# A small write and a wait on GpSimd in front of every indirect DMA of a graph network kernel

## The chip, the cores and the metric

The kernel runs on one core of a Trainium2 chip. The metric is the device time of one execution in microseconds (us). Before the change it is 4527.97 us, the median of three runs (4527.56 to 4528.97).

## What is computed

Four graph layers run one after the other on 6,250 nodes with 64 features and 200,000 edges; the edges come sorted by their target node. Each layer normalises its input and adds its result to `x`. Cut to what matters here:

```python
h = relu(layernorm(x)); Z = h @ W_shared.T; ze = he @ W_shared.T
a = Z[src] @ Wa_s.T + ze @ Wa_e.T + Z[dst] @ Wa_d.T       # one number per edge
H_all = einsum('ni,rio->nro', h, W_rel)                    # 16 relations
x = x + relu(segment_sum(H_all[src, rel] * a, dst))
h = relu(layernorm(x))
x = x + A @ relu(A @ h)            # A: sum over edges, two aggregations
h = relu(layernorm(x))
x = x + four_gcn_layers(h)         # four more aggregations, two dense pairs
h = relu(layernorm(x))
v_e = segment_sum(edge_attr, src) / max(count, 1)          # by SOURCE node
x = x + mlp(concat([h, v_e, u]))
```

## The kernel before

The work runs in five stages, and GpSimd's own work is almost only indirect DMAs.

1. **Setup.** TensorE computes the table `rel_table` (100,352 rows of 65 numbers: one row per node and relation) and SyncE stores it to device memory. GpSimd prepares two blocks of edge rows (`early_rows`).
2. **The edge loop.** The target nodes are cut in 391 groups of 16. TensorE sums group after group (`sum_group`, lines 1820 to 1832), from one-hot matrices that VectorE writes (lines 1350 and 1371); the same loop counts, for each pair of nodes, how many edges join them, and ScalarE stores these counts as the table `adjacency`. The rows of `rel_table` that the edges need are fetched by GpSimd: a round `r` is four gathers (`indirect_dma_start`, line 704), each of 128 rows, into a ring of 64 slots (`ring`, a part of the tile `ld_all`). There are 391 rounds, 1,564 gathers. Before round `r` GpSimd waits until group `r - 14` is summed (semaphore `summed`), so that its ring slots are free, and until the gathers of round `r - 2` have landed. VectorE needs round `g + 3` for group `g`. The ring therefore holds some nine rounds of lead. After the loop GpSimd writes the early rows to their places in `l3_sorted` (line 712, 64 indirect writes of 128 rows).
3. **Six aggregations.** `adjacency` is read back, in 13 pairs of halves for each aggregation, and multiplied with the node rows (line 1911); between them lie layer norms and two dense stages.
4. **Placing edge rows**, beside the aggregations and a part of stage 5. The fourth layer wants the edge rows by source node. The 200,000 rows come in blocks of 4,096: ScalarE and VectorE split a block in three bf16 parts (`split_high`, `split_middle`, `split_low`, lines 849 to 873), and GpSimd writes it with 32 indirect DMAs to computed places (line 730, 47 blocks, 1,499 writes; the last block has 27). GpSimd waits for `l3_split` before a block. Three buffers (`rows16`) take turns: ScalarE's `split_high` of block `m` waits until the writes of block `m - 3` have landed (`l3_moved`). ScalarE does these steps in fixed slots of its own program, between the copies of an aggregation's results, so a late write holds up the copies behind it.
5. **Node sums and the network.** The rows of `l3_sorted` are read back in two generations and summed by node (line 2029). The reading of the second generation waits for every placing write.

GpSimd's program is written out (no loop in it on this path), one instruction after the other. `Chain.link` adds one to a semaphore when its instruction is done and has the engine wait for that count before it goes on; the setup's instructions all use it. The tile `w_rel` holds the relation weights; its last reader is the computation of `rel_table`, and GpSimd waits for the storing of that table before its first gather.

Of the kernel before, what the change touches and what calls it, by code (L numbers as in the profile page):

```python
# [107 lines left out]
def build(nc, A, out):  # L108
# [3 lines left out]
    with ctx:  # L112
        def sb(name, shape, dt=f32):
            return ctx.enter_context(nc.sbuf_tensor(name, shape, dt))
# [30 lines left out]
        w_rel = sb("w_rel", [P, R, D])  # L145
# [183 lines left out]
        def s(name):  # L329
            if name not in S:  # L330
                S[name] = sem(name)
            return S[name]
# [290 lines left out]
        def _(pool):  # L623
            ch = Chain(pool, s("pool_chain"))
# [26 lines left out]
            def edge_pass(j):  # L651
# [5 lines left out]
                with pool.Fori(0, COUNT[j] // n) as i:  # L657
# [9 lines left out]
                    for k in range(n):  # L667
                        if name == "l3" and k % K == 0:
# [4 lines left out]
                                                (comb3[k] if name == "l3" else comb[k])[:, 0:width], None, compute_op=ALU.add,  # L673
                                                bounds_check=NROW - 1).then_inc(s(f"{fam}_scattered{k}"), 16)

            for n, (block, k0, cols, rows) in enumerate(early_rows):
                values = early_in[:, 0:cols * D48].rearrange("p (k d) -> p k d", d=D48)
                top = early_in[:, 0:cols * D48].bitcast(bf16).rearrange("p (k d two) -> p k d two", two=2, d=D48)[:, :, :, 1]
                pool.wait_ge(s("x_loaded"), 32 + 16 * (n + 1))
                pool.memset(rows[:, :, ONE:KEY], 1.0)  # L680
                for part in range(2):
                    ch.link(pool.tensor_copy(rows[:, :, part * D48:(part + 1) * D48], top))
                    ch.link(pool.tensor_tensor(values, values, rows[:, :, part * D48:(part + 1) * D48], ALU.subtract))
                pool.tensor_copy(rows[:, :, 2 * D48:3 * D48], top).then_inc(s("const_ready"), 1)
# [8 lines left out]
            with pool.If(flag1):  # L693
                pool.wait_ge(s("ring_ready"), 1)
                for r in range(ROUNDS):
                    if r * K == RING // 2:
                        pool.wait_ge(s("ring_ready"), 2)
                    if r >= AHEAD:
                        pool.wait_ge(s("summed"), r + TG - AHEAD)
                    if r >= 2:  # L700
                        pool.wait_ge(s(f"ring_in{r % 2}"), r // 2 * (16 * K))
                    pool.sem_inc(s("turn"), 1)
                    for c in range(r * K, r * K + K):
                        pool.indirect_dma_start(ring[:, c % RING, 0:TW], None, rel_table,  # L704
                                                bass.IndirectOffsetOnAxis(ap=rel_i[:, c:c + 1], axis=0)).then_inc(s(f"ring_in{r % 2}"), 16)
                pool.wait_ge(s("sorted_zeroed"), 16 * ZERO_DMAS)
                for block, k0, cols, rows in early_rows:
                    pool.wait_ge(s("l3_pos_ready"), block + 1)
                    pool.sem_inc(s("turn"), 1)
                    for k in range(cols):  # L710
                        at = block * SB_K + k0 + k
                        pool.indirect_dma_start(l3_sorted, bass.IndirectOffsetOnAxis(ap=l3_pos[:, at:at + 1], axis=0),
                                                rows[:, k, :], None).then_inc(s(f"l3_moved{block}"), 16)
            with pool.Else():
# [4 lines left out]
            with pool.If(flag2):  # L719
                pool.wait_ge(s("l3_pos_ready"), NSB + 1)  # L720
                for m in range(NSB + 1 - EARLY):
                    n = m + EARLY
                    q = m % 3
                    pool.wait_ge(s("l3_split"), m + 1)
                    if m < EARLY:
                        pool.wait_ge(s(f"l3_moved{m}"), 16 * SB_K)
                    pool.sem_inc(s("turn"), 1)
                    for k in range(SB_K if n < NSB else REST_DMAS):
                        parts = REST_TAIL if n == NSB and k == REST_K else P
                        pool.indirect_dma_start(l3_sorted, bass.IndirectOffsetOnAxis(ap=l3_pos[0:parts, n * SB_K + k:n * SB_K + k + 1], axis=0),  # L730
                                                rows16[q][0:parts, k, :], None).then_inc(s(f"l3_moved{q}"), 16)
            with pool.Else():
# [1343 lines left out]
```

## Time and profile before

| what | us |
|---|---|
| median of three runs | 4527.97 |
| span of the profiled execution | 6109.1 |
| its GpSimd busy time | 3104.2 |
| its TensorE busy time (matmul) | 3539.3 |
| its VectorE busy time | 2693.7 |

The profiled execution's span is the time from its first to its last instruction; no other time of that execution is recorded, and nothing is known of what lies around it. It is 1581.1 us (35%) longer than the median of the runs. Durations and orders are read from it, and the text says where that difference matters. "Issue" in a row is idle time for which the profile shows no releaser; a name behind an arrow is what ended the idle time.

### The profile page before, as it was taken

The numbers are of one execution on the slowest core, as the hardware profiler recorded it, in microseconds if no ns is written. First come the engines' busy times: TensorE is split into PE (matmuls) and PEld (weight loads), VectorE is DVE, ScalarE is ACT, GpSimd is POOL, SyncE is SP. The second block draws the span as 40 slices with busy tenths as digits, with TensorE's granted clock in tenths as the row PEclk, the third lists the DMA queues.
The fourth block names the chain that finished last, engine by engine and source line by source line (L and its number), as shares of the span: only waits on it lengthen the run. The fifth ranks groups of instructions, "written<-read, shape, count | busy, mean of one in ns | idle before, by whom it ended". The sixth has DMA issues, their size and how long they took to land.

```text
span 6109.1 us, 86298 instructions
## 1 busy us (share of the span) xinstructions
PE 3539.3 (58%) x18243; PEld 1786.5 (29%) x18244; DVE 2693.7 (44%) x9772; ACT 1506.8 (25%) x3741; POOL 3104.2 (51%) x3186
## 2 busy tenths in 40 slices
PE   5377777777776777776425455344654655451345
PEld 2133333333333333333202222122321223121333
DVE  6266666666666666666350110401202203015556
ACT  3132332323232323232111111111111111112552
POOL 2455555555555555555355656455255562555331
PEclk8588888888888888888656677676676775675668
DMA  5433333333333333333034444343143441342444
GB/s 181 105 77 79 77 77 77 79 77 78 77 79 77 82 73 79 77 77 76 25 114 148 149 140 168 127 137 125 58 167 129 155 154 61 128 157 93 158 153 111
DMA packets 599826, 650.58 MB, mean 106 GB/s; under 512 B 422854, under 2 KB 435892, under 8 KB 593429
## 3 DMA queue, kind: packets, MB, share of 16 engines
q1 hardware_dynamic: 382453, 463.07, 23.5%
q0 software_dynamic: 100064, 110.65, 8.6%
q10 hardware_dynamic: 117184, 75.50, 4.0%
q8 instruction: 42, 0.69, 0.0%
q14 instruction: 83, 0.68, 0.0%
HBM read 453.58 MB, written 192.06 MB: 106 GB/s over the span
## 4 chain that ended last, share of the span: by engine, by line
PE 38%; another core or an unknown queue 21%; issue 19%; DVE 11%; DMA 7%; ACT 2%; DVEq 1%; SPq 1%; POOL 0%; ACTq 0%; POOLq 0%
PE bank L1827 10%; PE bank L1828 7%; PE bank L1832 7%; PE bank L1911 7%; DMA ld_all<-adjacency 3%; DMA rel_table<-ld_all 2%; DVE hid_T L1652 2%; DMA rel_and_z<-adjacency 1%; DVE hid_T L1371 1%; PE bank L2029 1%; PE bank L1858 1%; DVE hid_T L1350 1%; PE bank L1961 1%; PE bank L1967 1%
## 5 line engine op out<-in xcount | busy, mean ns | idle before, releaser
L730 POOL DMA_INDIRECT l_sorted<-arena,l_pos x1499 | 1467.7, 979 | 1538.6 <-ACT arena L873 1057.8
L704 POOL DMA_INDIRECT ld_all<-rel_table,rel_and_z x1564 | 1537.4, 983 | 1158.3 <-remote 450.8
L1827 PE MATMUL bank<-hid_T 128*128 128x400 f16 x2346 | 974.6, 415 | 668.5 <-issue 549.4
L1828 PE MATMUL bank<-hid_T 128*128 128x384 f16 x2346 | 948.3, 404 | 28.7 <-issue 28.2
L1371 DVE TENSOR_SCALAR hid_T<-count_key,hid_T 128x400 f16<-128x400 int16 x2346 | 599.9, 326 | 744.9 <-remote 434.2
L1911 PE MATMUL bank<-rel_and_z,ld_all 128*128 128x512 fp8e4 (+1 forms) x1872 | 523.7, 419 | 524.7 <-issue 471.5
L1911 PE MATMUL bank<-ld_all 128*128 128x512 fp8e4 (+1 forms) x1950 | 504.6, 419 | 333.1 <-DMA ld_all<-adjacency 147.1
L1832 PE MATMUL bank<-ld_all,arena 128*32 x4692 | 519.6, 247 | 164.1 <-issue 163.3
L1827 PEld LDWEIGHTS bank<-hid_T 128*128 x2346 | 257.1, 110 | 1149.4 <-issue 1145.0
L793 ACT CAST ld_all<-bank 128x400 fp8e4<-128x400 f32 x391 | 191.1, 489 | 1595.4 <-remote 959.1
L1313 DVE COPY accT<-bank 128x512 f32<-128x512 f32 (+1 forms) x78 | 51.2, 657 | 1079.8 <-remote 593.1
L1832 PEld LDWEIGHTS bank<-ld_all,arena 128*32 128x32 f32 x4692 | 350.5, 122 | 413.2 <-issue 343.0
L1911 PEld LDWEIGHTS bank<-rel_and_z,ld_all 128*128 128x128 f16 x1872 | 186.8, 105 | 851.5 <-issue 704.0
L908 ACT COPY G<-bank 128x256 f32<-128x256 f32 (+1 forms) x78 | 28.1, 360 | 1508.2 <-remote 694.2
L1911 PEld LDWEIGHTS bank<-ld_all 128*128 128x128 f16 x1950 | 201.7, 109 | 610.3 <-issue 463.6
L1350 DVE TENSOR_SCALAR hid_T<-io,arena 128x256 f16<-128x256 f16 x1564 | 353.2, 292 | 0.1
L1828 PEld LDWEIGHTS bank<-hid_T 128*128 x2346 | 265.2, 113 | 203.6 <-issue 132.9
L2029 PE MATMUL bank<-ld_all,hid_T 128*128 128x145 bf16 x1188 | 130.4, 277 | 251.5 <-issue 105.5
L796 ACT ACTIVATE ld_all<-bank,minus_max 128x400 f16<-128x400 f32 x391 | 236.0, 603 | 0.0
L797 ACT ACTIVATE ld_all<-bank,minus_max 128x384 f16<-128x384 f32 x391 | 228.1, 583 | 0.0
L2029 PEld LDWEIGHTS bank<-ld_all,hid_T 128*128 128x128 bf16 x1188 | 110.5, 122 | 276.5 <-issue 276.4
L1264 DVE TENSOR_TENSOR dst_f<-dst_f,bank 128x512 f32<-128x512 f32 x96 | 60.3, 683 | 290.6 <-ACT arena L850 227.6
(302 smaller groups left out, 4366.0 us busy)
## 6 DMA issues: line engine op xcount, KB each, us to landing
ld_all<-adjacency SPq DMA_DIRECT2D x72, 1600.0 KB
rel_and_z<-adjacency SPq DMA_DIRECT2D x72, 1600.0 KB
l_sorted<-zeros SPq DMA_DIRECT2D x151, 424.0 KB
arena<-in_edge_attr SPq DMA_DIRECT2D x195, 256.0 KB
adjacency<-ld_all ACTq DMA_DIRECT2D x391, 100.0 KB
ld_all<-l_sorted SPq DMA_DIRECT2D x33, 1095.0 KB
rel_table<-ld_all SPq DMA_DIRECT2D x49, 520.0 KB, 3.6
ld_all<-rel_table,rel_and_z POOLq DMA_INDIRECT x1564
```

Source lines behind the costliest of these rows:

```text
L704: pool.indirect_dma_start(ring[:, c % RING, 0:TW], None, rel_table, bass.IndirectOffsetOnAxis(ap=rel_i[:, c:c + 1], axis=0)).then_inc(s(f" ...
L730: pool.indirect_dma_start(l3_sorted, bass.IndirectOffsetOnAxis(ap=l3_pos[0:parts, n * SB_K + k:n * SB_K + k + 1], axis=0), rows16[q][0:par ...
L793: act.copy(count_stage[:, 0:w0], b0[:, 0:w0], saturate=False)
L796: act.activation(over_junk[:, 0:w0], b0[:, 0:w0], ACT.Relu, bias=minus_max[:], accum_out=over[:, bass.ds(g * 2, 1)])
L797: act.activation(over_junk[:, w0:GW], b1[:, 0:GW - w0], ACT.Relu, bias=minus_max[:], accum_out=over[:, bass.ds(g * 2 + 1, 1)]).then_inc(s( ...
L1350: v.tensor_scalar(lo_ring[:, q * K + k, :], io256[:], lo_in[:, k0 + k:k0 + k + 1], None, ALU.is_equal)
L1371: v.tensor_scalar(pair_hot[q % 2][:, k, :], count_key[:], pair_in[q % 2][:, k:k + 1], None, ALU.is_equal)
L1827: pe.matmul(b0[:, 0:w0], low[:, 0:P], pair_hot[q % 2][:, k, 0:w0], start=k == 0, stop=k == CG - 1)
L1828: pe.matmul(b1[:, 0:GW - w0], low[:, P:2 * P], pair_hot[q % 2][:, k, 0:GW - w0], start=k == 0, stop=k == CG - 1)
L1832: ins = pe.matmul(half_sums[q // 4][:, q % 4 * TW:(q % 4 + 1) * TW], weights[q % 2][:, k, :], ring[:, bass.ds((first + k) & (RING - 1), 1) ...
L1911: ins = pe.matmul(bank[slot][:, 0:n * GN].rearrange("p (g d) -> p g d", d=GN), x16[:, t, :], a_half[side][:, 0:n, t // 2 * GN:(t // 2 + 1) ...
L2029: ins = pe.matmul(bank[n % 3][:, 0:KEY], node_hot[n % 2][:, k, :], sorted_in[n % 3][:, k, 0:KEY], start=k == 0, stop=k == CAPC[gen] - 1)
```

## The change

A function `pause` is added. It writes 16 zeros per partition into the first relation of `w_rel`, through `Chain.link`, so that GpSimd waits for its own write. It is called in front of each gather of the edge loop, each early placing write, and each placing write of the 47 blocks: 1,564 + 64 + 1,499 = 3,127 calls. The code of the other branches is untouched, and so are all other engines.

```diff
+            def pause():
+                ch.link(pool.memset(w_rel[:, 0:1, 0:16], 0))
+
...
                     for c in range(r * K, r * K + K):
+                        pause()
                         pool.indirect_dma_start(ring[:, c % RING, 0:TW], None, rel_table,
...
                     for k in range(cols):
                         at = block * SB_K + k0 + k
+                        pause()
                         pool.indirect_dma_start(l3_sorted, bass.IndirectOffsetOnAxis(ap=l3_pos[:, at:at + 1], axis=0),
...
                     for k in range(SB_K if n < NSB else REST_DMAS):
                         parts = REST_TAIL if n == NSB and k == REST_K else P
+                        pause()
                         pool.indirect_dma_start(l3_sorted, bass.IndirectOffsetOnAxis(ap=l3_pos[0:parts, n * SB_K + k:n * SB_K + k + 1], axis=0),
```

GpSimd's program in the edge loop, two rounds, before (`ld_all` is the ring; `rel_and_z` holds the row numbers; a wait in brackets stands in front of its instruction):

```order
89 L704 DMA ld_all<-rel_table,rel_and_z 128x65 [waits summed,ring_in1]
90 L704 DMA ld_all<-rel_table,rel_and_z 128x65 x3
91 L704 DMA ld_all<-rel_table,rel_and_z 128x65 [waits summed,ring_in0]
92 L704 DMA ld_all<-rel_table,rel_and_z 128x65 x3
```

and after, one round and the head of the next (`pool_chain` is the semaphore of `Chain.link`):

```order
169 L677 MEMSET w_rel 128x16 [waits summed,ring_in1]
170 L708 DMA ld_all<-rel_table,rel_and_z 128x65 [waits pool_chain]
171 L677 MEMSET w_rel 128x16
172 L708 DMA ld_all<-rel_table,rel_and_z 128x65 [waits pool_chain]
173 L677 MEMSET w_rel 128x16
174 L708 DMA ld_all<-rel_table,rel_and_z 128x65 [waits pool_chain]
175 L677 MEMSET w_rel 128x16
176 L708 DMA ld_all<-rel_table,rel_and_z 128x65 [waits pool_chain]
177 L677 MEMSET w_rel 128x16 [waits summed,ring_in0]
```

The round's own waits now stand in front of the first write of zeros, and every gather waits for the write before it.

GpSimd's program at a block of placing writes, before (`arena` holds the split rows, `l_pos` their places):

```order
880 L730 DMA l_sorted<-arena,l_pos 242176x146 [waits l3_split,l3_moved1]
881 L730 DMA l_sorted<-arena,l_pos 242176x146 x31
882 L730 DMA l_sorted<-arena,l_pos 242176x146 [waits l3_split]
```

and after:

```order
3405 L736 DMA l_sorted<-arena,l_pos 242176x146 [waits pool_chain]
3406 L677 MEMSET w_rel 128x16 [waits l3_split,l3_moved1]
3407 L736 DMA l_sorted<-arena,l_pos 242176x146 [waits pool_chain]
3408 L677 MEMSET w_rel 128x16
3409 L736 DMA l_sorted<-arena,l_pos 242176x146 [waits pool_chain]
```

What stood as 32 DMAs in a row is now 32 pairs of a write and a DMA.

## Rows read from the trace of the kernel before

**Rows 1.** The page: head, engine totals, 40 slices, shares of the chain.
```profile
span 6109.1 us, 86298 instructions
...
PE 3539.3 (58%) x18243; PEld 1786.5 (29%) x18244; DVE 2693.7 (44%) x9772; ACT 1506.8 (25%) x3741; POOL 3104.2 (51%) x3186
...
PE   5377777777776777776425455344654655451345
...
POOL 2455555555555555555355656455255562555331
PEclk8588888888888888888656677676676775675668
...
PE 38%; another core or an unknown queue 21%; issue 19%; DVE 11%; DMA 7%; ACT 2%; DVEq 1%; SPq 1%; POOL 0%; ACTq 0%; POOLq 0%
```

**Rows 2.** GpSimd's groups: busy us, mean ns, idle before, its releasers.
```profile
L704 POOL DMA_INDIRECT ld_all<-rel_table,rel_and_z x1564 | 1537.4, 983 | 1158.3 <-remote 450.8 <-issue 401.5 <-PE bank L1832 305.2
L730 POOL DMA_INDIRECT l_sorted<-arena,l_pos x1499 | 1467.7, 979 | 1538.6 <-ACT arena L873 1057.8 <-issue 480.7
L712 POOL DMA_INDIRECT l_sorted<-h,l_pos x32 | 31.3, 977 | 10.4 <-issue 10.4
```

**Rows 3.** Timeline of GpSimd: the first gather and the last placing write.
```profile
201.75 1.16 POOL L704 DMA_INDIRECT ld_all<-rel_table,rel_and_z  x1 [3.35 <-issue]
...
5982.03 0.90 POOL L730 DMA_INDIRECT l_sorted<-arena,l_pos  x1 [0.31 <-issue]
```

**Rows 4.** Engines' busy time in three stretches of one aggregation.
```profile
core 0: us, PE busy (x) PEld busy (x) DVE busy (x) ACT busy (x) POOL busy (x), PEclk, DMA share, GB/s
3950.00:3980.00 30.00, 25.77 (x123) 12.32 (x122) 5.06 (x8) 7.49 (x10) 13.91 (x15) 0.97 0.73 261
3990.00:4040.00 50.00, 11.88 (x23) 2.50 (x21) 4.37 (x7) 7.52 (x10) 38.10 (x40) 0.53 0.15 45
4060.00:4090.00 30.00, 28.21 (x135) 13.49 (x133) 5.06 (x8) 8.40 (x12) 4.85 (x5) 0.98 0.73 256
```

**Rows 5.** Timeline of TensorE, the same aggregation.
```profile
3961.66 5.56 PE L1911 MATMUL bank<-ld_all 128*128 128x512 fp8e4 x25
...
4016.91 0.58 PE L1911 MATMUL bank<-rel_and_z,ld_all 128*128 128x512 fp8e4 x1 [2.21 <-issue]
4019.71 0.58 PE L1911 MATMUL bank<-rel_and_z,ld_all 128*128 128x512 fp8e4 x1 [2.22 <-issue]
```

**Rows 6.** GpSimd's groups from 500 to 2500 us, in the edge loop.
```profile
L704 POOL DMA_INDIRECT ld_all<-rel_table,rel_and_z x1154 | 1135.5, 984 | 863.4 <-remote 333.2 <-issue 293.7 <-PE bank L1832 236.6
```

**Rows 7.** GpSimd's waits at the placing writes: us in total, times, longest.
```profile
POOL l_sorted L730 <- ACT arena L873: 1057.8, 42, 100.2
```

**Rows 8.** Timeline of the edge loop, 1508 to 1516 us.
```profile
1508.40 1.49 DVE L1371 TENSOR_SCALAR hid_T<-count_key,hid_T 128x400 f16<-128x400 int16 x6 [2.41 <-remote]
...
1509.18 1.06 POOL L704 DMA_INDIRECT ld_all<-rel_table,rel_and_z  x1 [2.21 <-remote]
...
1510.54 0.99 POOL L704 DMA_INDIRECT ld_all<-rel_table,rel_and_z  x1 [0.30 <-issue]
1510.63 0.95 DVE L1350 TENSOR_SCALAR hid_T<-io,arena 128x256 f16<-128x256 f16 x4
...
1511.84 0.94 POOL L704 DMA_INDIRECT ld_all<-rel_table,rel_and_z  x1 [0.30 <-issue]
...
1513.09 0.95 POOL L704 DMA_INDIRECT ld_all<-rel_table,rel_and_z  x1 [0.31 <-issue]
```

**Rows 9.** Timeline of GpSimd's setup, every instruction waited for.
```profile
2.44 0.20 POOL L633 MEMSET ones<- 128x128 f32 x1
2.71 0.10 POOL L634 MEMSET minus_max<- 128x1 f32 x1
2.87 0.47 POOL L635 IOTA count_key<- 128x400 int16 x1
```

## Prediction, made before the changed kernel was run

> **What bounds the kernel now.** I read the page first. No engine is full: TensorE 58%, GpSimd 51%, VectorE 44% of the span [rows 1]. But the span is 6109.1 us and the median of the runs 4527.97. That is the main difficulty here: GpSimd's busy 3104 us are half of the one and 69% of the other. So I ask next whether the profiled execution has delays that cannot all be in a timed run. It has: "another core or an unknown queue" holds 21% of the chain that ended last (1283 us), and "issue" 19% [rows 1].
>
> The engines' busy time by stretch shows where. Between 3990 and 4040 us GpSimd issues placing writes without a pause (40 in 50 us), and TensorE gets only 23 matmuls through, though in the 30 us before and in 30 us soon after it does 123 and 135 [rows 4]. Its timeline shows matmuls 2.8 us apart, each after 2.2 us of "issue", where it did 25 in 5.56 us before [rows 5]. The DMA engines are at 0.15 then and cannot be full. The reader is to see that GpSimd keeps its pace (40 in 50 us is one in 1.25) while TensorE loses it. Whether these delays belong to the recording or to the chip no row tells; the 1581 us by which the timed runs are shorter say that most of them are absent there. I go by that.
>
> Last I read GpSimd's groups. A gather takes 0.983 us, a placing write 0.979, an early one 0.977 [rows 2]. Behind one another they stand 0.30 us apart [rows 8], so GpSimd needs 1.28 us for each. This pace is the same inside and outside the delayed stretches. If it holds in a timed run, then:
>
> - before the first gather: 201.75 us [rows 3]
> - 1,564 + 64 + 1,499 = 3,127 DMAs x 1.28 = 4003 us
> - behind the last placing write, 6109.1 - 5982.9 = 126 us [rows 1, 3]
> - sum 4331 us.
>
> The timed runs take 4528. Only 197 us are left for all of GpSimd's waits. In the profiled execution they were far more: it waits in the edge loop, where a round of four gathers comes every 2000 / (1154 / 4) = 6.93 us [rows 6] against 4 x 1.28 = 5.12 of its own, and 42 times for 1057.8 us at ScalarE's split, 25 us each [rows 7]. Take TensorE's delays away, and just these two waits shrink. My reading is that the timed kernel is paced by GpSimd's row of DMAs, in the loop and in the placing, though the profile shows it half idle.
>
> **The change, part by part.** It adds 3,127 writes of zeros with a wait, and removes and moves nothing else. The trace before has no such write between two DMAs, so I bound it. A memset of one element per partition takes 0.10 us, of 128 elements 0.20 [rows 9]; by a line through both, 16 elements take 0.11. In the setup, where each instruction is waited for, the next begins 0.06 to 0.07 us after the end [rows 9]. The 0.30 us in front of a DMA exist already [rows 8].
>
> - Least: the write disappears in those 0.30 us, so 0.
> - Middle: 0.07 us behind the DMA, 0.11 for the write, then the same 0.30, so +0.18.
> - Most: 0.30 on both sides of the write, so +0.41. A still larger cost would need the lock of the third rival.
>
> I take +0.18, since rows show each piece of it. On GpSimd alone that is 3,127 x 0.18 = 563 us (0 to 1282). By part:
>
> - Edge loop: 1,564 x 0.18 = 282 us; a round goes from 5.12 to 5.84 us. Queued behind the pause stand the gathers, and behind these VectorE's adding of the source term, the weights and TensorE's group sum. The ring's lead of nine rounds covers a few late rounds, not 391 of them.
> - Early writes: 64 x 0.18 = 12 us, behind the last gather, while the loop's tail and the second flag are computed (GpSimd waits there anyway); free, or 12.
> - Placing: 1,499 x 0.18 = 270 us; a block goes from 41 to 46.7 us. Behind a late block stand ScalarE's `split_high` three blocks on, then the copies of aggregation results behind it in ScalarE's program, and with them TensorE.
>
> What hides a part of it are the 197 us of waits. Some cannot shrink: the wait for the second flag, and the last block's wait for its split. I take half, 100 us, as giving way. Sum: 4528 + 563 - 100 = 4991. With all 197 absorbed it is 4894, with none 5091. Against the profiled execution's own span the same sum comes out near nothing: 5.84 is under 6.93 and 46.7 is under 41 + 25, so there all pauses but those of the last block (27 x 0.18 = 5 us) lie in idle time. Its span should stay near 6109, or fall if TensorE's delays follow the density of GpSimd's DMAs.
>
> **A rule against the rows.** In the loop a gather that starts while VectorE writes its six count one-hots takes 1.06 us, one beside no such work 0.94 [rows 8]. The sum uses the means, which hold that 0.1 already. The Trainium skill, "SBUF — State Buffer", section "Who interferes with whom", says that a VectorE instruction in a 2-port mode and a GpSimd instruction shut each other out of the shared port for the whole instruction. [...] By that rule a gather beside these instructions would wait for them, and the row's 0.1 us does not bear that out for a gather; a write of zeros no row shows.
>
> **The rivals.**
>
> 1. *The pause lies under cover (chance 0.17).* If everything in a timed run is shorter than in the trace by the same factor, 4528 / 6109 = 0.74, then the relations of the profile hold: GpSimd waits a quarter of every round, and the pauses fill that. Price: the last block alone, 5 us by the trace's durations, so 4533, no change. For it speaks the idle time in rows 6 and 7; against it that nothing shows a DMA of GpSimd below 0.94 us.
> 2. *Fewer delays on the other side (0.13; the one that is faster).* Suppose that TensorE's slow stretches [rows 4, 5] are in part in the timed runs, and come from GpSimd's DMAs standing too close. The pause would thin them from one in 1.28 us to one in 1.46. This can only pay if GpSimd's own pace is shorter in a timed run, so that TensorE and not GpSimd sets the end. A tenth of the 1283 us of unknown waits, 128 us, would give 4400. It decides from the point where the delays that go exceed the 0.18 us per DMA that GpSimd adds. Against it: by the trace's durations only 197 us can be had at all.
> 3. *The write waits for VectorE (0.07).* In a round VectorE has two stretches of such work, 1.49 and 0.95 us [rows 8]. If two of four writes fall into them and wait half of each, a round costs 0.75 + 0.48 = 1.2 us more, 391 x 1.2 = 480 on top: 4991 + 480 = 5471. This is the case that the Trainium skill's rule of the section named above would give for a write. Against it: the gathers beside the same stretches lose 0.1 us.
>
> **How the numbers follow.** Forecast, GpSimd paces and the pause is paid for: 0.63. With rival 3 that makes slower by over 0.2%: 0.70. Same: 0.17. Faster: 0.13. (0.2% is about what a measurement of this kernel can tell from no change.) Predicted time 4990. The forecast's own range, from a pause of 0.05 to one of 0.3 us, is 4528 + 156 - 100 = 4584 to 4528 + 938 - 0 = 5466. The range should leave out the faster case and the far end of a 0.41 us pause, and take in rival 1: 4515 to 5450.
>
> **What the next profile would show.** Right, if: the writes of zeros stand at 0.1 to 0.15 us, 3,127 of them; two DMAs of GpSimd begin about 1.46 us apart; GpSimd's idle time at the gathers and placing writes shrinks by as much as the writes add, with the span of the profiled execution hardly longer; and the timed runs come nearer to the span. Wrong, if: DMAs still begin 1.28 us apart (no cost), the DMA itself grows or shrinks behind a pause (then the sum is off in its main term), writes beside lines 1350 and 1371 take a microsecond (rival 3), or TensorE's matmuls of line 1911 are no longer spread in the bursts and the timed runs are shorter (rival 2). The forecast falls as a whole if the time stays within 10 us of 4528 while the distance between DMAs has grown: then GpSimd did not pace the timed kernel.

## The result, and the profile after

The changed kernel takes 4781.11 us (median of four runs, 4779.42 to 4785.0) against 4528.47 before: 252.6 us more, a ratio of 1.0557 (95% interval 1.0542 to 1.0572). I had forecast 4990, slower.

First the page of the changed kernel: head, engine totals, GpSimd's slices, TensorE's clock, shares of the chain that ended last, by engine and by line. In the changed kernel a gather is line 708, a block write line 736, the write of zeros line 677.

```profile
span 4780.5 us, 89425 instructions
...
PE 3231.5 (68%) x18243; PEld 1682.0 (35%) x18244; DVE 2770.8 (58%) x9772; ACT 1514.4 (32%) x3741; POOL 3498.2 (73%) x6313
...
POOL 2377777877787778777877777777757777577760
PEclk8699999998999999999967978688588785795778
...
POOL 44%; PE 19%; issue 16%; DVE 10%; DMA 7%; ACT 2%; DVEq 2%; POOLq 0%; SPq 0%; ACTq 0%
POOL l_sorted L736 24%; POOL ld_all L708 13%; PE bank L1833 5%; POOL w_rel L677 5%; PE bank L1838 4%; PE bank L1834 3%; DMA ld_all<-rel_table,rel_and_z 3%; DMA rel_table<-ld_all 2%; DVE hid_T L1658 2%; POOL l_sorted L717 1%; DVE hid_T L1377 1%; PE bank L1967 1%; PE bank L2035 1%; PE bank L1973 1%; DMA ld_all<-l_sorted 1%
```

GpSimd is busy in 73% of the span and holds 44% of the chain; in [rows 1] it held 0%. The span, 4780.5 us, lies 1.7 us below that run's own time. So this profile shows the timed kernel, while the one I predicted from (span 6109.1) did not: its execution was disturbed. The kernel before was therefore profiled twice more. One of these pages, to be held against [rows 1]:

```profile
span 4528.7 us, 86298 instructions
...
POOL 2377777777777777777667777777657777577650
...
PE 29%; POOL 23%; issue 12%; DVE 10%; DMA 3%; ACT 2%; DVEq 1%; SPq 0%; POOLq 0%; ACTq 0%
POOL l_sorted L730 22%; PE bank L1827 9%; PE bank L1832 6%; PE bank L1828 5%; PE bank L1911 2%; DVE hid_T L1652 2%; PE bank L1961 1%; PE bank L2029 1%; PE bank L1967 1%; DMA ld_all<-l_sorted 1%; DMA ld_all<-adjacency 1%; PE bank L1858 1%; DVE hid_T L1371 1%; DVE G L1520 0%; DVE hid_T L1350 0%
```

The span is 4528.7 us (the third one's 4524.2). GpSimd holds 23% of the chain, "another core or an unknown queue" nothing. Of the 23%, 22 are block writes (line 730), and the gathers of line 704 are not listed; in the changed kernel the gathers hold 13%. All comparisons below use this second profile of before.

Waits for other work, in total us, times and longest, of the kernel before (answering to [rows 7]) and of the changed one. The first line of each is ScalarE's wait for the placing writes, in front of `split_high`:

```profile
ACT arena L862 <- DMA l_sorted<-arena,l_pos: 293.1, 17, 29.7
...
POOL l_sorted L730 <- ACT arena L873: 132.9, 9, 43.6
...
POOL ld_all L704 <- PE bank L1832: 38.7, 39, 2.2
POOL ld_all L704 <- DMA ld_all<-rel_table,rel_and_z: 36.6, 120, 0.3
```

```profile
ACT arena L868 <- DMA l_sorted<-arena,l_pos: 489.8, 22, 33.5
...
POOL w_rel L677 <- ACT arena L879: 86.6, 6, 32.2
...
POOL ld_all L708 <- PE bank L1838: 11.6, 43, 0.3
```

The placing is later for ScalarE: it waits 489.8 us for placing writes where it waited 293.1. These rows do not give GpSimd's slack. A gap of 0.30 us stands in front of every DMA; the 120 waits for earlier gathers, 36.6 us, are this gap and nothing more, and some long waits stand under "issue". The slack is what is left of the span when GpSimd's own work is taken off. Before, that is 200.2 us up to the first gather, 3037.0 of DMAs, 3,127 x 0.30 = 938.1 of gaps and 109.8 behind the last write, 4285.1 in all; 243.6 us are left. The prediction had 197.

After the change the same terms are 202.3, 3050.8, 3,127 x 0.28 = 875.6 and 107.9, and the writes of zeros add 409.1, 4645.7 in all; 134.8 are left. So GpSimd's own work grew by 361 us, and 109 us of slack gave way.

GpSimd's groups of the second profile (busy us, mean ns, idle before), against [rows 2], and those of the changed kernel:

```profile
L704 POOL DMA_INDIRECT ld_all<-rel_table,rel_and_z x1564 | 1500.7, 960 | 560.9 <-issue 485.6 <-PE bank L1832 38.7 <-DMA ld_all<-rel_table,rel_and_z 36.6
L730 POOL DMA_INDIRECT l_sorted<-arena,l_pos x1499 | 1472.8, 983 | 599.0 <-issue 466.0 <-ACT arena L873 132.9
```

```profile
L708 POOL DMA_INDIRECT ld_all<-rel_table,rel_and_z x1564 | 1516.8, 970 | 461.2 <-POOL w_rel L677 407.2 <-issue 40.6 <-PE bank L1838 11.6
L736 POOL DMA_INDIRECT l_sorted<-arena,l_pos x1499 | 1471.1, 981 | 441.3 <-POOL w_rel L677 411.9 <-issue 29.4
L677 POOL MEMSET w_rel<- 128x16 f32 x3127 | 409.1, 131 | 92.1 <-ACT arena L879 86.6 <-DMA rel_table<-ld_all 2.6
```

The timeline of GpSimd in a block of placing writes (start, length, work, idle before), before and after:

```profile
3000.05 0.97 POOL L730 DMA_INDIRECT l_sorted<-arena,l_pos  x1 [0.31 <-issue]
3001.32 0.97 POOL L730 DMA_INDIRECT l_sorted<-arena,l_pos  x1 [0.30 <-issue]
```

```profile
2999.72 0.97 POOL L736 DMA_INDIRECT l_sorted<-arena,l_pos  x1 [0.28 <-POOL w_rel L677]
3000.69 0.12 POOL L677 MEMSET w_rel<- 128x16 f32 x1
3001.09 0.97 POOL L736 DMA_INDIRECT l_sorted<-arena,l_pos  x1 [0.28 <-POOL w_rel L677]
```

From one DMA to the next are 1.37 us, where it was 1.27. The write begins when the DMA ends, takes 0.12, and the next DMA begins 0.28 after it. The prediction had 1.46.

When the gathers and the blocks' writes began (least, median and longest time in ns, then the starts of the first and the last), and how long VectorE waited for gathers (us, times), before and after:

```profile
L704 POOL DMA_INDIRECT ld_all<-rel_table,rel_and_z x1564: 942/947/1286, 200.2 to 2257.5; - x196
...
  DVE rel_and_z L1356: 14.7, 6
...
L730 POOL DMA_INDIRECT l_sorted<-arena,l_pos x1499: 903/972/2871, 2358.8 to 4418.0; - x188
```

```profile
L708 POOL DMA_INDIRECT ld_all<-rel_table,rel_and_z x1564: 949/952/1348, 202.3 to 2390.2; - x196
...
  DVE rel_and_z L1362: 173.4, 81
...
L736 POOL DMA_INDIRECT l_sorted<-arena,l_pos x1499: 905/974/3277, 2482.0 to 4671.7; - x188
```

| stretch, first start to last start | before | after | difference |
|---|---|---|---|
| up to the first gather | 200.2 | 202.3 | +2.1 |
| gathers | 2057.3 | 2187.9 | +130.6 |
| early writes, second flag | 101.3 | 91.8 | -9.5 |
| blocks' writes | 2059.2 | 2189.7 | +130.5 |
| behind the last write | 110.7 | 108.8 | -1.9 |

The sum is 251.8 us, the whole difference. Half lies in the edge loop, half in the placing. In the loop VectorE now waits 173.4 us for gathers, where it waited 14.7.

Two stretches of 50 us of the changed kernel in which GpSimd issues all the time, to be held against the middle one of [rows 4]:

```profile
core 0: us, PE busy (x) PEld busy (x) DVE busy (x) ACT busy (x) POOL busy (x), PEclk, DMA share, GB/s
2985.00:3035.00 50.00, 29.46 (x165) 16.90 (x163) 5.16 (x9) 9.87 (x14) 39.98 (x73) 0.81 0.50 155
3900.00:3950.00 50.00, 28.10 (x114) 13.22 (x114) 4.97 (x8) 9.47 (x15) 39.98 (x73) 0.74 0.41 123
```

TensorE gets 165 and 114 matmuls through where the disturbed execution had 23.

TensorE's granted clock also fell, from a mean of 0.867 (0.97 between 500 and 2200 us) to 0.839 (0.93). In the loop this cannot be the cause, since GpSimd's own work fills the longer round almost by itself (below). In the placing what the lower clock costs was not tried apart.

### The profile page after: what moved, and what is told of

It is laid out like the page before. It is cut to its first block, busy times and chain, and to the rows that moved or that the text cites. A ratio compares the mean times of both kernels' runs of the same rounds, so it can differ in the third digit from the quotient of the medians.

```text
span 4780.5 us, 89425 instructions
## 1 busy us (share of the span) xinstructions
PE 3231.5 (68%) x18243; PEld 1682.0 (35%) x18244; DVE 2770.8 (58%) x9772; ACT 1514.4 (32%) x3741; POOL 3498.2 (73%) x6313
## 4 chain that ended last, share of the span: by engine, by line
POOL 44%; PE 19%; issue 16%; DVE 10%; DMA 7%; ACT 2%; DVEq 2%; POOLq 0%; SPq 0%; ACTq 0%
POOL l_sorted L736 24%; POOL ld_all L708 13%; PE bank L1833 5%; POOL w_rel L677 5%; PE bank L1838 4%; PE bank L1834 3%; DMA ld_all<-rel_table,rel_and_z 3%; DMA rel_table<-ld_all 2%; DVE hid_T L1658 2%; POOL l_sorted L717 1%; DVE hid_T L1377 1%; PE bank L1967 1%; PE bank L2035 1%; PE bank L1973 1%; DMA ld_all<-l_sorted 1%
## 5 line engine op out<-in xcount | busy, mean ns | idle before, releaser
L708 POOL DMA_INDIRECT ld_all<-rel_table,rel_and_z x1564 | 1516.8, 970 | 461.2 <-POOL w_rel L677 407.2
L1833 PE MATMUL bank<-hid_T 128*128 128x400 f16 x2346 | 861.2, 367 | 386.7 <-DVE arena L1386 253.3
L1834 PE MATMUL bank<-hid_T 128*128 128x384 f16 x2346 | 830.3, 354 | 0.0
L1377 DVE TENSOR_SCALAR hid_T<-count_key,hid_T 128x400 f16<-128x400 int16 x2346 | 674.8, 355 | 25.8 <-PE bank L1838 15.2
L1917 PE MATMUL bank<-ld_all 128*128 128x512 fp8e4 (+1 forms) x1950 | 475.2, 408 | 188.5 <-DMA ld_all<-adjacency 114.3
L1833 PEld LDWEIGHTS bank<-hid_T 128*128 x2346 | 236.1, 101 | 879.4 <-issue 873.1
L677 POOL MEMSET w_rel<- 128x16 f32 x3127 | 409.1, 131 | 92.1 <-ACT arena L879 86.6
L1917 PE MATMUL bank<-rel_and_z,ld_all 128*128 128x512 fp8e4 (+1 forms) x1872 | 410.2, 378 | 78.8 <-DMA rel_and_z<-adjacency 78.8
L1834 PEld LDWEIGHTS bank<-hid_T 128*128 x2346 | 239.3, 102 | 112.8 <-issue 33.3
L1926 PE MATMUL bank<-work,accT 128*128 128x64 f32 x588 | 83.5, 288 | 240.5 <-DVE accT L1319 240.5
L1270 DVE TENSOR_TENSOR dst_first<-dst_first,bank 128x512 f32<-128x512 f32 x90 | 56.4, 682 | 274.5 <-ACT arena L856 274.3
```

Source lines behind the costliest of these rows:

```text
L677: ch.link(pool.memset(w_rel[:, 0:1, 0:16], 0))
L1377: v.tensor_scalar(pair_hot[q % 2][:, k, :], count_key[:], pair_in[q % 2][:, k:k + 1], None, ALU.is_equal)
L1833: pe.matmul(b0[:, 0:w0], low[:, 0:P], pair_hot[q % 2][:, k, 0:w0], start=k == 0, stop=k == CG - 1)
L1834: pe.matmul(b1[:, 0:GW - w0], low[:, P:2 * P], pair_hot[q % 2][:, k, 0:GW - w0], start=k == 0, stop=k == CG - 1)
L1917: ins = pe.matmul(bank[slot][:, 0:n * GN].rearrange("p (g d) -> p g d", d=GN), x16[:, t, :], a_half[side][:, 0:n, t // 2 * GN:(t // 2 + 1) ...
```

## The experiments

All times are medians; "before" is 4527.5 to 4528.5 in each set.

### The kernel before, once more

No edit.

> The kernel before, unchanged, once more with its profile. Theory (the long span of its first profile, 6109 us, comes with the recording, and GpSimd's dense DMAs bring it about): the time is 4528 us and the profile is again far longer, over 5500 us, with TensorE's matmuls of line 1911 some 2 to 3 us apart while GpSimd writes. Rival (that first profile was a chance event): the span is within 30 us of the time, and TensorE's matmuls stand close.

4529.5 us (ratio 1.0003, 0.9993 to 1.0013) and a span of 4528.7. The theory that the long span comes with every recording of this kernel fell; the rival held. A later look for the same question:

> The kernel before, unchanged, for a third profile. Theory (the first profile's 6109 us were an event of that one execution, the second had 4528.7): the span is within 20 us of 4528. Rival (it recurs in some of the profiled executions): over 5500.

One run of 4525.98 us, span 4524.2. Of three profiled executions of before one was long; what disturbed it stays open.

### Where the pause costs: gathers alone, writes alone

```diff
# gathers alone: pause() only here
                     for c in range(r * K, r * K + K):
+                        pause()
# writes alone: pause() only in the two loops of placing writes
```

> The pause in front of the 1,564 gathers alone. In the changed kernel a pause adds 0.10 us between two DMAs (1.28 to 1.38). Theory (GpSimd paces both the loop and the placing): 1,564 x 0.10 = 156 us less a little slack, 4528 + 140 = 4670 us. Rival (only the placing is paced by GpSimd, the loop by VectorE and TensorE): 4528 to 4540. Rival (only the loop is): 4528 + 253 = 4780.

4639.63 us, +111.5 (ratio 1.0241, 1.0224 to 1.0258).

> The pause in front of the 1,563 placing writes alone (early ones and blocks). Theory (GpSimd paces both): 1,563 x 0.10 = 156 us less the waits that give way, some 40: 4528 + 115 = 4643 us. Rival (only the loop is paced by GpSimd): 4528 to 4540. Rival (only the placing): 4780.

4663.75 us, +135.6 (ratio 1.0301, 1.0284 to 1.0319). Both stages pay, the gathers less than the 140 us expected, the writes more than the 115; the parts sum to 247 of the 253 us. Neither rival, that a single stage pays, holds. With the pause at the gathers alone the loop's stretch grows by 133.5 us (2190.8 against 2057.3), and some of that comes back before the end.

### Two pauses in a row

```diff
+                ch.link(pool.memset(w_rel[:, 0:1, 0:16], 0))
                 ch.link(pool.memset(w_rel[:, 0:1, 0:16], 0))
```

> Two pauses in a row in front of each of the 3,127 DMAs. The second costs its write, 0.12 us, and the gap of 0.07 us between two chained instructions, with nothing left to hide it: +0.19 us each. Theory (GpSimd paces throughout): 4781 + 3,127 x 0.19 = 5375 us. Rival (a pause only shifts DMAs, the number does not count): 4781 to 4850. Rival (the chained write is longer in a pair because of VectorE's lock): over 5500.

5320.42 us (ratio 1.1751, 1.1732 to 1.1771), 539 above the changed kernel: 0.172 us for each second pause, against 0.081 for each first. Timeline of GpSimd:

```profile
3000.63 0.98 POOL L737 DMA_INDIRECT l_sorted<-arena,l_pos  x1 [0.28 <-POOL w_rel L678]
3001.61 0.13 POOL L677 MEMSET w_rel<- 128x16 f32 x1
3001.79 0.11 POOL L678 MEMSET w_rel<- 128x16 f32 x1
3002.18 0.98 POOL L737 DMA_INDIRECT l_sorted<-arena,l_pos  x1 [0.28 <-POOL w_rel L678]
```

DMAs stand 1.55 us apart. The second write adds its 0.11 and the 0.05 between the two. The distance grows by 0.18 (1.55 less 1.37), near the expected 0.19. Part is still absorbed: GpSimd's wait for ScalarE's split falls from 86.6 to 37.9 us.

### Write without wait, wait without write

```diff
 # no wait: the write waits for the one before it, the DMA for nothing
-                ch.link(pool.memset(w_rel[:, 0:1, 0:16], 0))
+                pool.wait_ge(s("pool_chain"), ch.base + ch.k)
+                ch.also(pool.memset(w_rel[:, 0:1, 0:16], 0))
 # wait alone
-                ch.link(pool.memset(w_rel[:, 0:1, 0:16], 0))
+                pool.sem_inc(s("pool_chain"), 1)
+                ch.k += 1
+                pool.wait_ge(s("pool_chain"), ch.base + ch.k)
```

> The 3,127 writes stay, but the DMA behind one no longer waits for it; each write waits only for the write before it, which has long been done. Theory (what a pause costs is the write's own 0.125 us in GpSimd's row, and the 0.27 us in front of the DMA are there with or without a wait): 4781 us within 10. Rival (the wait costs its part): under 4740. Rival (the DMA overlaps the write): 4528 to 4600.

> No writes: GpSimd's queue adds one to the semaphore itself and waits for that count, in front of each of the 3,127 DMAs. Theory (the wait lies inside the 0.30 us that stand between two DMAs anyway): 4528 to 4545 us, DMAs still 1.26 to 1.28 us apart. Rival (a wait alone costs some 0.05 us each): 4528 + 150 = 4680 or more.

The write without its wait: 4541.38 us, +13.9 (ratio 1.0031, 1.002 to 1.0043). The wait without a write: 4530.88, +3.4 (ratio 1.0005, 0.9996 to 1.0014). For the first, the theory of 4781 fell and the rival of an overlap (4528 to 4600) held; for the second the theory held, and its 3.4 us are not clear of noise. Neither half costs much alone. The second is not the same wait: here GpSimd's queue raises the count itself, in the pause the finished write does. Timelines of GpSimd, without wait, then without write:

```profile
3001.58 0.97 POOL L737 DMA_INDIRECT l_sorted<-arena,l_pos  x1 [0.18 <-issue]
3002.55 0.12 POOL L678 MEMSET w_rel<- 128x16 f32 x1
3002.86 0.97 POOL L737 DMA_INDIRECT l_sorted<-arena,l_pos  x1 [0.18 <-issue]
```

```profile
3001.57 0.97 POOL L738 DMA_INDIRECT l_sorted<-arena,l_pos  x1 [0.31 <-POOLq L677]
3002.85 0.97 POOL L738 DMA_INDIRECT l_sorted<-arena,l_pos  x1 [0.30 <-POOLq L677]
```

Both keep 1.27 to 1.28 us from DMA to DMA. The DMA begins 0.30 us after a DMA, but 0.18 after a write that it does not wait for, so a write of 0.12 is free: 0.12 + 0.18 = 0.30. If it waits for the write, the gap is 0.28 again. The 0.10 us that a pause adds from DMA to DMA are what the wait takes away again (0.28 less 0.18).

### A wide write, with and without the wait

```diff
-                ch.link(pool.memset(w_rel[:, 0:1, 0:16], 0))
+                ch.link(pool.memset(w_rel[:, 0:4, :], 0))        # or the form without a wait
```

> The changed kernel with a wider write: 256 zeros per partition in place of 16, waited for as before. By the rows of the setup (0.10 us for 1 element, 0.20 for 128) the write takes about 0.31 us in place of 0.125. Theory (what is waited for stands in GpSimd's row in full): 4781 + 3,127 x 0.185 = 5360 us. Rival (the cost is that of the wait, whatever the write's length): 4781 to 4800.

> The same wide write, but the DMA behind it does not wait for it. With the small write and no wait, the write lay inside the 0.30 us between two DMAs and cost 14 us in all. Theory (these 0.30 us are the start of the next DMA, and run beside whatever GpSimd does meanwhile): 0.31 us of writing just fills them, DMAs 1.28 to 1.35 us apart, 4540 to 4700 us. Rival (the start of the DMA begins when the write is done): as with the wait, over 5200.

With the wait 5366.04 us (ratio 1.1848, 1.183 to 1.1866), 6 us from the theory; the rival fell. Without it 5048.58 (ratio 1.1153, 1.1136 to 1.117), between theory and rival: both missed. Timelines, with the wait, then without:

```profile
3000.66 0.98 POOL L736 DMA_INDIRECT l_sorted<-arena,l_pos  x1 [0.28 <-POOL w_rel L677]
3001.64 0.33 POOL L677 MEMSET w_rel<- 128x256 f32 x1
3002.24 0.98 POOL L736 DMA_INDIRECT l_sorted<-arena,l_pos  x1 [0.28 <-POOL w_rel L677]
```

```profile
3001.48 0.97 POOL L737 DMA_INDIRECT l_sorted<-arena,l_pos  x1 [0.17 <-issue]
3002.45 0.33 POOL L678 MEMSET w_rel<- 128x256 f32 x1
3002.94 0.97 POOL L737 DMA_INDIRECT l_sorted<-arena,l_pos  x1 [0.17 <-issue]
```

The write takes 0.33 us. Then come 0.27 to 0.28 us with the wait and 0.16 to 0.17 without, close to the 0.28 and 0.18 of the small write. So the write stands in GpSimd's row in full, and what is saved is a nearly fixed 0.12 to 0.14 us (0.30 less 0.16 to 0.18), not everything that fits in 0.30. The two kernels differ by 317 us in 3,127 pauses: the wait costs 0.101 us each. Together the distance from DMA to DMA is

- before: 0.97 + 0.30 = 1.27
- small write, no wait: 0.97 + 0.12 + 0.18 = 1.27
- small write, wait: 0.97 + 0.12 + 0.28 = 1.37
- wide write, no wait: 0.97 + 0.33 + 0.16 = 1.46
- wide write, wait: 0.98 + 0.33 + 0.27 = 1.58

### One pause in a round, one in eight writes

```diff
+                        if c % K == 0:
+                            pause()
...
+                        if k % 8 == 0:
+                            pause()
```

> Pauses (with their wait) only in front of the first gather of each round (391) and of every eighth placing write. Theory (in the loop GpSimd has 0.17 us of slack per round before it paces, and one pause adds 0.12): the loop costs nothing, the placing 196 x 0.11 = 22 us less slack: 4540 to 4552. Rival (each pause costs its 0.08 us wherever it stands): 4528 + 587 x 0.08 = 4575.

4544.74 us, +16.8 (ratio 1.0035, 1.0022 to 1.0049), as the theory had it and 30 below the rival. 588 pauses ran. In its profile the loop with 391 of them has a stretch of 2058.1 us, 0.8 more than before, and the block writes 2072.7, 13.5 more: the slack of a round takes up one pause, and the placing pays. So GpSimd does not pace the loop before the change.

### Fewer DMAs: how close do the others follow?

```diff
# half the writes (waits on l3_moved halved)
-                    for k in range(SB_K if n < NSB else REST_DMAS):
+                    for k in range(0, SB_K if n < NSB else REST_DMAS, 2):
# and half the gathers (waits on ring_in halved)
-                    for c in range(r * K, r * K + K):
+                    for c in range(r * K, r * K + K, 2):
```

Both leave out work: half of the edge rows never reach their places, and the second also sums old rows of the ring. Their results are not the layer's; only their times count here.

> The kernel before, but every second placing write is left out (early ones too), and so half of the edge rows never reach their places; waits are on half the counts. No pauses. Theory (GpSimd paces the placing, 2059 us from the first to the last block's write): GpSimd's own work there falls to half, and the end is set by TensorE, ScalarE and the reads of adjacency; from their rows I take about 400 us off, 4130 (4000 to 4300). Rival (another engine paces that stretch as closely): over 4450.

> As the last one, and every second gather of the edge loop is left out too (the ring's other slots keep what they held). Theory (in the loop a round takes 5.26 us, GpSimd's own four gathers 5.05, and VectorE is 85% and TensorE 86% busy, so they stand close behind): some 50 to 150 us less than the kernel with half the placing writes. Rival (the loop is paced by GpSimd alone): 500 us less or more. Rival (not by GpSimd): within 10 us of it.

Half the writes: 4293.27 us (ratio 0.9492, 0.9477 to 0.9506). Page, head and chain:

```profile
span 4280.5 us, 85517 instructions
...
PE 42%; DMA 14%; DVE 13%; issue 6%; ACT 2%; DVEq 1%; SPq 0%; ACTq 0%; POOL 0%
PE bank L1911 12%; PE bank L1827 10%; DMA ld_all<-adjacency 9%; PE bank L1832 7%; PE bank L1828 6%; DMA rel_and_z<-adjacency 3%; DVE hid_T L1652 2%; PE bank L2029 1%; PE bank L1961 1%; PE bank L1967 1%; PE bank L1858 1%; DVE hid_T L1371 1%; DMA ld_all<-l_sorted 1%; DVE work L1280 1%; DVE G L1520 1%
```

GpSimd is gone from the chain, and the stretch of the block writes shrinks from 2059.2 to 1806.4 us. The gain, 234 us, is not the 400 I had estimated, though just inside the range given: TensorE's aggregations (line 1911, 12%) and the reads of `adjacency` (9 + 3%) follow closer. Half the gathers too: 4283.74 us (0.9458, 0.9442 to 0.9473), only 9.5 us below, less than the spread of either kernel's runs. The theory of 50 to 150 us fell; the rival held, that GpSimd does not pace the loop before the change. The gathers' row and GpSimd's wait for TensorE there:

```profile
L704 POOL DMA_INDIRECT ld_all<-rel_table,rel_and_z x782: 942/988/1170, 201.4 to 2242.3; - x196
```

```profile
POOL ld_all L704 <- PE bank L1832: 1099.7, 367, 4.7
```

With half its work gone and 1100 us of waiting, the loop still takes 2040.9 us, 5.22 for a round. Between 500 and 2200 us TensorE is 86% busy there and VectorE 83%, so these two hold the pace; which of them more was not tried.

## Why the prediction was right, and where its sizes were off

**The pacing.** The main step, that GpSimd's row of DMAs sets the timed kernel though the profile showed it half idle, was right for the placing and only half right for the loop. For the placing, halving the writes takes 234 us off. For the loop, halving the gathers takes some 10 us off, no more. Before the change GpSimd's own work in a round is (1500.7 + 1,564 x 0.30) / 391 = 5.04 us. The other engines need 5.22, measured with half the gathers, and a little more with all of them, since VectorE's one-hots are slower then (below). The round took 2057.3 / 391 = 5.26. After the change GpSimd's own work is (1516.8 + 1,564 x (0.131 + 0.28)) / 391 = 5.52, and the round 5.60: now GpSimd paces. So of the 0.48 us that a round's four pauses add, 0.34 reach the end. That the claim about the loop did so little harm is luck: the other engines' pace lies only 0.18 us above GpSimd's, less than four pauses add.

**The cost of a pause** was the term that was mis-sized: 0.18 us taken. From DMA to DMA 0.10 are typical. The mean over all is 361 / 3,127 = 0.115, since some writes and gathers are slower beside other work (write 0.131 in the mean, gathers 0.970 after 0.960); the end time grew by 0.08 for each. Of the three pieces the write was right (0.11 taken, 0.12 to 0.13 measured). The 0.07 us behind the DMA is not there: the write begins as the DMA ends. And the gap in front of the DMA is 0.28, not 0.30. With the measured mean the sum is 361 less the 109 that gave way, 252, and the measured increase 253; the prediction had 563 less 100. The bounds, 0 and 0.41, held the pause.

**The slack.** 197 us of waits were worked out from a disturbed profile and the median; the undisturbed profile leaves 244. The difference is in the gathers (0.983 us in the disturbed execution, 0.960 in the second profile) and in the time behind the last write (126 against 110). A placing write took 0.979 us against 0.983, and their distance of 1.28 us was sound too. This is why the sum could be made at all.

**What gave way.** I let 100 us of 563 be absorbed, and 109 of 361 were. In the loop the pauses add 190 us (2159.6 of own work after 1969.9), of which 130.6 reach the end and 59 are absorbed. In the blocks they add 165, of which 130.5 reach the end and 34 are absorbed. The early writes add 6, and the stretch they stand in took 9.5 us less. That the 100 came so near is partly luck: half of the waits was a choice between none and all, with no row behind it.

**The profiled span** did not stay near 6109: the second and the third profile of before show that figure to have been one execution's own. The prediction's reading that the delays of [rows 4, 5] are mostly absent in timed runs was right; that the pause could thin them (rival 2) has nothing to act on: the kernel without pauses has no such delays. The chance of 0.13 for "faster" had this as its only ground.

**Rival 1** (all under cover) fell: the spans of the second and third profile lie 2 us below those runs' own times, and GpSimd's durations in them are what the first trace said, not 0.74 of it. That nothing shows a DMA below 0.94 us was misread: [rows 3] has a placing write of 0.90. **Rival 3** (the write waits for VectorE) fell as a price of a microsecond: the write's mean is 0.131 us. There is a small effect the other way round. VectorE's count one-hots, from 500 to 1500 us (count, busy us, mean ns), before, after, and with the wide write:

```profile
L1371 DVE TENSOR_SCALAR hid_T<-count_key,hid_T 128x400 f16<-128x400 int16 x1117 | 300.4, 337 | 49.1 <-PE bank L1832 42.8 <-issue 3.4
```

```profile
L1377 DVE TENSOR_SCALAR hid_T<-count_key,hid_T 128x400 f16<-128x400 int16 x1068 | 306.3, 354 | 12.3 <-PE bank L1838 8.2 <-issue 1.0
```

```profile
L1377 DVE TENSOR_SCALAR hid_T<-count_key,hid_T 128x400 f16<-128x400 int16 x936 | 304.5, 391 | 2.7 <-PE bank L1838 0.2
```

From 337 over 354 to 391 ns: with GpSimd's write a one-hot takes 17 ns more in the mean, with the longer write 54. It is the write that does it and not the wait: the mean is 336 with the wait alone and 359 with the write alone. The gathers do it too: with half of them it is 320. The Trainium skill, "SBUF — State Buffer", section "Who interferes with whom", has a VectorE instruction in a 2-port mode and a GpSimd instruction shut each other out for the whole instruction. The direction agrees; whether the one-hots run in such a mode no run here shows. The small change of the mean would fit instructions that meet only now and then, which was not looked at. Whether it is part of the 14 us of the write without a wait was not tried apart.

No version that does the whole work beats the kernel before. That GpSimd's DMAs do not pace the loop, but do pace the placing, points to fewer or cheaper placing writes; it was not tried with a full result.

## What to carry to other kernels

If the span of a profile and the median of the runs differ by more than a few us, profile again before reasoning from shares: here one disturbed execution showed an engine idle half of the time that was in fact the pace of half of the kernel. Where only such a profile is at hand, sum one engine's durations and fixed distances and hold the sum against the median; 4331 of 4528 us told more than any share. To find what a stage is worth, take work out of the engine under suspicion as well as putting some in: an engine with 0.18 us of slack in 5.2 looks like the pace when it is loaded, and shows that it is not when it is relieved.

## What the runs showed of the hardware

- A write of GpSimd between two indirect DMAs costs its length, but the DMA behind it starts 0.12 to 0.14 us earlier than behind another DMA (0.16 to 0.18 against 0.30). A write of 0.12 us without a wait is therefore free from DMA to DMA.
- Waiting on the engine's own write costs 0.10 us (317 us for 3,127 waits, with the wide write). A wait on a count that the queue itself has just raised cost 3.4 us for 3,127, which is not clear of noise.
- A gather or a block write, an indirect DMA of 128 rows, took 0.96 to 1.00 us in the mean in every variant, disturbed execution included.
- VectorE's one-hots lengthen beside GpSimd's work: in the mean from 500 to 1500 us 320 ns with half the gathers, 336 to 337 with all, 354 to 359 with small writes, 391 with wide ones.
